# Channel attention through the channel products of the normalised image instead of through queries and keys of every pixel

## The chip, the cores and the metric

The kernel runs on one core of a Trainium2 chip. The metric is the time of one execution on the device, in microseconds. The kernel is one program of four layers that run one after the other on the same core; the change touches the third of them, `layer2`.

## The reference, cut to what matters

```python
# x: 8 images, 384 channels, 32 x 32 pixels; four layers, each x = x + layer(_gn(x)); this is the third
def _L2_conv_ref(x, w_qkv, temperature, w_out, b_out):
    xt = x.reshape(b, c, n).transpose(0, 2, 1)              # n = 1024 pixels, c = 384
    q, k, v = jnp.split(xt @ w_qkv, 3, axis=-1)
    q = q.reshape(b, n, h, d).transpose(0, 2, 1, 3)         # h = 8 heads, d = 48
    k = k.reshape(b, n, h, d).transpose(0, 2, 3, 1)
    v = v.reshape(b, n, h, d).transpose(0, 2, 1, 3)
    q = q / jnp.maximum(jnp.sqrt(jnp.sum(q * q, axis=-2, keepdims=True)), 1e-12)
    k = k / jnp.maximum(jnp.sqrt(jnp.sum(k * k, axis=-1, keepdims=True)), 1e-12)
    k = k * temperature
    attn = jax.nn.softmax(jnp.einsum('bhpn,bhnq->bhpq', k, q), axis=-1)   # 48 x 48 per head
    out = jnp.einsum('bhnp,bhpq->bhnq', v, attn)
    out = out.transpose(0, 2, 1, 3).reshape(b, n, c) @ w_out + b_out
    return out.transpose(0, 2, 1).reshape(b, c, H, W)
```

The attention is over channels. All that it takes from queries and keys are three sets of sums over the pixels: k with q, k with k, and q with q, head by head. `_gn` is a group normalisation without weights (32 groups); its mean and scale for each channel come from sums that the layer before has left in `stat`.

## The kernel before, in words

`layer2` starts with `norm_params`, which turns `stat` into a mean and a scale for each channel (`gn`), while SyncE loads image 0 and the weights (`begin`) and GpSimd clears tiles (`fill`). Then the main block goes through the 8 images. Everything is float32. The 384 channels lie as 3 groups of 128 partitions (`G3`); an image is 1024 pixels, 8 chunks of 128 (`NT`).

For each image, in the order of the data:

- VectorE normalises `xs` into `h` (L645, three instructions).
- TensorE projects (`project`, L838): for each chunk of pixels and for keys and queries in turn, three matmuls of 384 columns into one of four PSUM banks `p_a`. That is a "fill", 16 of them an image; ScalarE copies each to `kq` (L811). TensorE waits for the copy of fill i-4 before fill i.
- TensorE sums over the pixels (L849): for each head 8 matmuls of `kq` with itself, 112 columns wide (k in columns 0 to 47, q in 64 to 111), into `gram` in the two banks `p_g`.
- VectorE takes the diagonals of kk and qq (L743, L745, L749), a matmul with ones (L854) spreads the query sums, ScalarE takes square roots (L817, L819), VectorE divides and scales (L752 to L767), and the softmax follows (L770 to L778, with ScalarE's exponential at L822).
- TensorE transposes the 8 small matrices (L859), mixes them with `w_out` (L870, two steps for each half), and multiplies with the value weights (L877) to `f`, a 384 x 384 matrix for this image. VectorE copies the stages out of PSUM (L780, L784, L788).
- TensorE applies `f` to `h` (L885, 18 matmuls of 512 columns), VectorE adds bias and residual into `xo` (L793) and leaves the sums for the next layer (L798). SyncE stores `xo`.

The order on TensorE is written out by hand: while the attention chain of image b runs on the other engines, the projection of image b+1 is fed in between, cut at `BEFORE` = 3, 9, 11 and 12 fills. The loop runs over pairs of images with two buffers each for `xs` and `h`. In the last turn it wraps around, so the normalisation and projection of image 0 are made once more and not used. The load of image b+1 is issued on SyncE only when the previous image has been written to `xo` (L717), since it takes over its buffer, and VectorE normalises image b+1 at the head of turn b (L735 to L737), ahead of the attention chain of image b. `Arena.loop_sem` is a semaphore that starts at one, for waits in a hardware loop; `sem_inc` on `tick` counts and nothing waits for it.

Of the kernel before, what the change touches and what calls it, by code (L numbers as in the profile page):

```python
# [654 lines left out]
def layer2(nc, sh, x, w_qk, w_vT, w_out, temp, b_out, y):  # L655
# [5 lines left out]
    yv = y.rearrange("b (g p) n -> p b g n", p=P)  # L661
    with Arena(nc, "c") as a:
        xs = a.sb("xs", [P, 2, G3, N])
        h = a.sb("h", [P, 2, G3, N])
# [24 lines left out]
        s_sub, s_an, s_tt, s_te, s_m, s_me, s_f, s_fe, s_o, s_oe, s_st = (
            a.loop_sem(n) for n in ("sub", "an", "tt", "te", "m", "me", "f", "fe", "o", "oe", "st"))  # L690
        a.open()


        BEFORE = (3, 9, 11, 12)
        def begin(e):
            e.dma_start(xs[:, 0, :, :], xv[:, 0, :, :]).then_inc(s_x[0].sem, 16)
            e.dma_start(w[:], w_qk.rearrange("(g p) s n -> p g s n", p=P)).then_inc(s_w.sem, 16)
# [3 lines left out]
            e.dma_start(bo[:], b_out.rearrange("(g p) -> p g", p=P), allow_slow_non_contiguous=True).then_inc(s_w.sem, 16)  # L701

        def fill(e):
            e.memset(kq[:], 0.0).then_inc(s_z.sem, 1)
            e.memset(ones[:], 1.0).then_inc(s_z.sem, 1)
            e.memset(m[:], 0.0).then_inc(s_z.sem, 1)
            e.wait_ge(s_z.sem, s_z.at(3))

        norm_params(nc, sh, "n2", p_a[0], begin, fill)
        with nc.Block() as block:  # L710

            @block.sync
            def _(e):
                with e.Fori(0, B // 2) as b2:
                    for u in range(2):
                        b = b2 * 2 + u
                        e.wait_ge(s_oe.sem, s_oe.at(b * 6))  # L717
                        e.sem_inc(sh["tick"], 1)
                        e.dma_start(xs[:, 1 - u, :, :].unsqueeze(1), xv[:, ds((b + 1) % B, 1), :, :]).then_inc(s_x[1 - u].sem, 16)
                        e.wait_ge(s_oe.sem, s_oe.at(b * 6 + 6))  # L720
                        e.dma_start(yv[:, ds(b, 1), :, :], xo[:].unsqueeze(1)).then_inc(s_y.sem, 16)
                        e.wait_ge(s_y.sem, s_y.at((b + 1) * 16))
                        e.sem_inc(s_yd.sem, 1)
                for u in range(2):
                    e.wait_ge(s_x[u].sem, s_x[u].at(16 * (B // 2 + 1 - u)))

            @block.vector
            def _(e):
                e.wait_ge(s_x[0].sem, s_x[0].at(16))
                normalise(e, sh, h[:, 0, :, :], xs[:, 0, :, :], 0).then_inc(s_h.sem, 1)  # L730
                e.wait_ge(s_w.sem, s_w.at(80))
                with e.Fori(0, B // 2) as b2:
                    for u in range(2):
                        b = b2 * 2 + u
                        e.wait_ge(s_x[1 - u].sem, s_x[1 - u].at((b2 + 1 + u) * 16))  # L735
                        e.wait_ge(s_o.sem, s_o.at(b * 6))
                        normalise(e, sh, h[:, 1 - u, :, :], xs[:, 1 - u, :, :], (b + 1) % B).then_inc(s_h.sem, 1)  # L737

                        e.wait_ge(s_g.sem, s_g.at(b + 1))
                        idk = sh["ident"][0:D, 0:D].unsqueeze(1).broadcast_to([D, 4, D])  # L740
                        idq = sh["ident"][64:TP, 64:TP].unsqueeze(1).broadcast_to([D, 4, D])
                        for v in range(2):
                            e.tensor_tensor(dq[64:TP, 4 * v:4 * v + 4, :], gram[64:TP, v, :, 64:TP], idq, ALU.mult).then_inc(s_dq.sem, 1)  # L743
                        for v in range(2):
                            last = e.tensor_tensor(dk[:, 4 * v:4 * v + 4, :], gram[0:D, v, :, 0:D], idk, ALU.mult)  # L745
                        last.then_inc(s_c.sem, 1)
                        e.wait_ge(s_c.sem, s_c.at(b * 5 + 1))
                        e.sem_inc(sh["tick"], 1)
                        e.tensor_reduce(rk[:], dk[:], AX, ALU.add).then_inc(s_dq.sem, 1)  # L749

                        e.wait_ge(s_sq.sem, s_sq.at(b * 2 + 1))
                        e.tensor_scalar(rk[:], rk[:], 1e-12, None, ALU.max)  # L752
                        e.wait_ge(s_sq.sem, s_sq.at(b * 2 + 2))
                        e.tensor_scalar(rq[:], rq[:], 1e-12, None, ALU.max).then_inc(s_c.sem, 1)
                        e.wait_ge(s_c.sem, s_c.at(b * 5 + 2))
                        e.sem_inc(sh["tick"], 1)
                        e.reciprocal(rk[:], rk[:])
                        e.reciprocal(rq[:], rq[:]).then_inc(s_c.sem, 1)
                        e.wait_ge(s_c.sem, s_c.at(b * 5 + 3))
                        e.sem_inc(sh["tick"], 1)  # L760
                        e.tensor_tensor(rk[:], rk[:], tmp[:], ALU.mult)
                        for v in range(2):
                            last = e.tensor_tensor(at2[:, 4 * v:4 * v + 4, :], gram[0:D, v, :, 64:TP], rq[:, 4 * v:4 * v + 4, :], ALU.mult)
                        last.then_inc(s_c.sem, 1)
                        e.wait_ge(s_c.sem, s_c.at(b * 5 + 4))
                        e.sem_inc(sh["tick"], 1)
                        e.tensor_tensor(at2[:], at2[:], rk[:].unsqueeze(2).broadcast_to([D, HEADS, D]), ALU.mult).then_inc(s_c.sem, 1)  # L767
                        e.wait_ge(s_c.sem, s_c.at(b * 5 + 5))
                        e.sem_inc(sh["tick"], 1)
                        e.tensor_reduce(mx[:], at2[:], AX, ALU.max).then_inc(s_sub.sem, 1)  # L770
                        e.wait_ge(s_sub.sem, s_sub.at(b * 4 + 1))
                        e.tensor_tensor(at2[:], at2[:], mx[:].unsqueeze(2).broadcast_to([D, HEADS, D]), ALU.subtract).then_inc(s_sub.sem, 1)
                        e.wait_ge(s_ex.sem, s_ex.at(b + 1))
                        e.tensor_reduce(mx[:], at2[:], AX, ALU.add).then_inc(s_sub.sem, 1)
                        e.wait_ge(s_sub.sem, s_sub.at(b * 4 + 3))
                        e.reciprocal(mx[:], mx[:]).then_inc(s_sub.sem, 1)
                        e.wait_ge(s_sub.sem, s_sub.at(b * 4 + 4))
                        e.tensor_tensor(at2[:], at2[:], mx[:].unsqueeze(2).broadcast_to([D, HEADS, D]), ALU.mult).then_inc(s_an.sem, 1)  # L778
                        e.wait_ge(s_tt.sem, s_tt.at(b + 1))
                        e.tensor_copy(attT[:].rearrange("p h d -> p (h d)"), p_m[0:D, 0, 0:C]).then_inc(s_te.sem, 1)  # L780
                        for v in range(PAIRS):
                            e.wait_ge(s_m.sem, s_m.at(b * 4 + v + 1))
                            for r in (0, 64):
                                last = e.tensor_copy(m[r:r + D, v, :], p_m[r:r + D, v % 2, 0:C])  # L784
                            last.then_inc(s_me.sem, 1)
                        for g in range(G3):
                            e.wait_ge(s_f.sem, s_f.at(b * 3 + g + 1))
                            e.tensor_copy(f[:, g, :], p_a[g][:, 0:C]).then_inc(s_fe.sem, 1)  # L788
                        e.wait_ge(s_yd.sem, s_yd.at(b))
                        for i in range(2 * G3):  # L790
                            g, n = i // 2, i % 2
                            e.wait_ge(s_o.sem, s_o.at(b * 6 + i + 1))
                            e.scalar_tensor_tensor(xo[:, g, n * HALF:(n + 1) * HALF], p_a[i % 4][:], bo[:, g:g + 1],  # L793
                                                   xs[:, u, g, n * HALF:(n + 1) * HALF], ALU.add, ALU.add).then_inc(s_oe.sem, 1)
# [8 lines left out]
            def _(e):  # L803
                def leave(n, steps):

                    for i in steps:
                        c, s = i // 2, i % 2
                        e.wait_ge(s_a.sem, s_a.at(n * (2 * NT) + i + 1))
                        if i == 0:
                            e.wait_ge(s_g.sem, s_g.at(n))  # L810
# [1703 lines left out]
```

## Time and profile before

| | |
|---|---|
| median of 3 runs | 6763.02 us (6761.66 to 6776.2) |
| profiled execution | 6760.66 us, its span 6758.4 us |
| TensorE matmul busy, whole span | 5974.2 us (88%) |
| `layer2`, from its first instruction to that of the layer after it | 5641.9 to 6327.4 us of the span |
| TensorE matmul busy in one image of `layer2` (5766.8 to 5845.3) | 74.03 of 78.50 us |
| VectorE, ScalarE busy in the same image | 25.70, 12.50 us |

All times within the span are in microseconds from its start. A float32 matmul stands in the trace as two instructions, so the 48 matmuls of a projection are x96; a transpose stands as one. Matmuls are pipelined: the duration of one is longer than the distance to the next.

### The profile page before, as it was taken

Reading aid. Unit: us, or ns where it says so; the run is one execution under the profiler, and the core shown is the slowest. Engines: PE = TensorE matmul, PEld = TensorE weight load, DVE = VectorE, ACT = ScalarE, POOL = GpSimd, SP = SyncE. Lnnn points to the kernel's source line nnn. Section 1 sums busy time; section 2 is a strip of 40 time slices with the busy share of each in tenths; the row PEclk is TensorE's granted clock in tenths of the full one; section 3 lists DMA queues with packets and bytes.
Section 4 is the critical chain, followed back from the end, with each engine's and each line's share of the span. In section 5 each row is a group of like instructions: output and inputs, shape, how many; then the busy total and the mean of one; then the engine's idle time right before and its main releaser. Section 6 shows DMA issues by size and latency. Waiting matters only on the chain. (4 is left out here: it accounts for less than half of the span.)

```text
span 6758.4 us, 123692 instructions
## 1 busy us (share of the span) xinstructions
PE 5974.2 (88%) x46612; PEld 4080.9 (60%) x46612; DVE 4837.0 (72%) x10092; ACT 3924.4 (58%) x5363; POOL 783.3 (12%) x780
## 2 busy tenths in 40 slices
PE   5999999999968989988889889898898996999798
PEld 2554454445425558865578755688556884555598
DVE  6877787788755779877788777888678893333333
ACT  3766676676633558865578755787556882111242
POOL 2212222221220011000020100100101100000000
PEclk9999999999989989999989999999998998999899
DMA  4111112111114545545355544454545552101598
GB/s 141 45 53 55 40 48 58 54 39 43 45 58 118 117 103 127 120 104 122 88 133 123 121 103 109 115 126 107 124 103 121 115 121 78 38 37 56 125 231 200
DMA packets 198795, 652.65 MB, mean 97 GB/s; under 512 B 61769, under 2 KB 68865, under 8 KB 155315
## 3 DMA queue, kind: packets, MB, share of 16 engines
q1 hardware_dynamic: 178147, 606.02, 36.5%
q0 software_dynamic: 19968, 37.78, 2.1%
q8 instruction: 400, 6.55, 0.4%
q14 instruction: 280, 2.29, 0.1%
HBM read 539.94 MB, written 65.59 MB: 90 GB/s over the span
## 5 line engine op out<-in xcount | busy, mean ns | idle before, releaser
L2330 PE MATMUL b_p<-b_work,b_hkt 64*128 64x144 f32 (+37 forms) x27520 | 2113.6, 309 | 257.1 <-DVE b_acc L2201 148.9
L2330 PEld LDWEIGHTS b_p<-b_work,b_hkt 64*128 64x128 f32 x27520 | 1964.9, 195 | 482.2 <-DVE b_work L2276 282.9
L2276 DVE TENSOR_TENSOR b_work<-b_work 128x140 f32<-128x140 f32 (+26 forms) x5312 | 1610.5, 356 | 230.1 <-PE b_p L2330 175.9
L2171 ACT ACTIVATE b_work<-b_work,b_mcol 128x512 f32<-128x512 f32 (+6 forms) x1328 | 764.8, 647 | 1025.3 <-DVE b_work L2276 886.0
L530 ACT ACTIVATE a_ex<-a_p_t 128x1024 f32<-128x1024 f32 x512 | 523.8, 1023 | 420.0 <-PE a_p_t L466 417.4
L2175 ACT ACTIVATE b_work<-b_work,b_mrow 128x544 f32<-128x544 f32 (+6 forms) x1328 | 762.1, 645 | 0.0
L2201 DVE SCALAR_TENSOR_TENSOR b_acc<-b_p,b_dwc,b_acc 128x323 f32<-128x323 f32 (+14 forms) x1088 | 624.2, 577 | 184.2 <-PE b_p L2330 184.2
L596 DVE TENSOR_REDUCE a_nm<-a_p_x 128x1 f16<-128x1024 f32 x512 | 624.8, 1220 | 147.4 <-PE a_p_x L455 138.5
L1742 PE MATMUL b_p<-b_hp,b_ow 128*98 128x512 f32 x1568 | 723.5, 612 | 0.0
L602 DVE TENSOR_TENSOR a_el<-a_ex,a_eh 128x1024 f16<-128x1024 f32 x512 | 680.7, 1330 | 6.7 <-ACT a_eh L535 6.7
L535 ACT CAST a_eh<-a_ex 128x1024 f16<-128x1024 f32 x512 | 535.5, 1046 | 54.7 <-ACT a_ex L530 3.0
L2210 DVE SCALAR_TENSOR_TENSOR b_acc<-b_p,b_dwc,b_acc 128x1024 f32<-128x1024 f32 x384 | 491.4, 1280 | 91.3 <-PE b_p L2330 89.7
L2178 ACT ACTIVATE b_work<-b_work 128x1792 f32<-128x1792 f32 (+2 forms) x332 | 530.9, 1599 | 0.0
L1742 PEld LDWEIGHTS b_p<-b_hp,b_ow 128*98 128x98 f32 x1568 | 251.5, 166 | 398.7 <-issue 394.0
L466 PE MATMUL a_p_t<-a_q,a_kh 97*128 97x512 f16 x1024 | 393.7, 384 | 34.0 <-ACT a_ex L530 34.0
L484 PE MATMUL a_p_o<-a_eh,a_v 128*112 128x512 f16 x1024 | 397.9, 389 | 26.8 <-DVE a_osum L590 19.3
L2180 ACT ACTIVATE b_work<-b_work 128x736 f32<-128x736 f32 (+13 forms) x332 | 396.0, 1193 | 0.0
L484 PE MATMUL a_p_o<-a_el,a_v 128*112 128x512 f16 x1024 | 394.8, 386 | 0.0
L455 PE MATMUL a_p_x<-a_kh,a_q 96*128 96x512 f16 x1024 | 315.9, 390 | 88.8 <-DVE a_nm L596 88.1
L466 PE MATMUL a_p_t<-a_q,a_kl 96*128 96x512 f16 x1024 | 393.4, 384 | 0.0
L1770 POOL TENSOR_TENSOR b_off<-b_off,b_grid 18x512 f32<-18x512 f32 (+2 forms) x56 | 79.4, 1418 | 2262.8 <-DVE b_mx L1763 2262.8
L1739 PE MATMUL b_p<-b_halves,b_ows 128*114 128x512 f16 (+1 forms) x1360 | 325.3, 391 | 13.9 <-DVE b_halves L1834 10.1
(212 smaller groups left out, 6059.0 us busy)
## 6 DMA issues: line engine op xcount, KB each, us to landing
b_work<-sampling_positions SPq DMA_DIRECT2D x666, 512.0 KB, 6.5
d_win<-merged_kernels SPq DMA_DIRECT2D x192, 263.0 KB, 7.0
b_xin<-x SPq DMA_DIRECT2D x24, 1024.0 KB, 9.6
a_xr<-in_x SPq DMA_DIRECT2D x12, 1536.0 KB, 10.0
x<-a_xr SPq DMA_DIRECT2D x9, 1536.0 KB, 6.1
c_xs<-x SPq DMA_DIRECT2D x9, 1536.0 KB, 6.4
b_xr<-x SPq DMA_DIRECT2D x13, 1024.0 KB, 18.8
x<-b_xr SPq DMA_DIRECT2D x13, 1024.0 KB, 4.7
```

The lines of the kernel that those rows point to most:

```text
L466: last = e.matmul(p_t[:, n, :], kk[0:r, hd, c * P:(c + 1) * P], q[0:r, hd, n * HALF:(n + 1) * HALF], start=(r > MAXROW), stop=(r == MAXROW))
L484: last = e.matmul(bank[0:TP, :], v[:, c, hh % HEADS, :], part[:, k % WR, n * HALF:(n + 1) * HALF], start=(c == 0 and r == 0), stop=(c == N ...
L535: e.copy(eh[:, m % WR, :], ex[:, m % ER, :]).then_inc(s_e.sem, 1)
L596: e.tensor_reduce(nm[:, k // NT % 4, k % NT:k % NT + 1], p_x[:].rearrange("p a n -> p (a n)"), AX, ALU.max, negate=True).then_inc(s_m.sem, 1)
L602: e.tensor_tensor(el[:, k % WR, :], ex[:, k % ER, :], eh[:, k % WR, :], ALU.subtract).then_inc(s_l.sem, 1)
L1742: last = e.matmul(bank_of(u[1])[0:M, :].rearrange("p (a b) -> p a b", b=W), ow[:, k * M:(k + 1) * M], hp[:, s, r0:r0 + 16, c0:c0 + W], sta ...
L2171: last = e.activation(rx[:, u, xo[c]:xo[c + 1]].rearrange("p (a b) -> p a b", a=H), pp[:, b, 1, :].rearrange("p (a b) -> p a b", a=H)[:, : ...
L2175: last = e.activation(ry[:, u, yo[c]:yo[c + 1]], pp[:, b, 0, first_row * W:end * W], ACT.Abs, bias=mrow[:, c:c + 1])
L2178: e.activation(rx[:, u, 0:xo[SIDE]], rx[:, u, 0:xo[SIDE]], ACT.Relu, bias=1.0, scale=-1.0).then_inc(tp.s_rx.sem, 1)
L2201: e.scalar_tensor_tensor(total, G, dwc[:, g, tap:tap + 1], total, ALU.mult, ALU.add).then_inc(tp.s_g.sem, 1)
L2276: e.tensor_tensor(S[:, k % NS, 0:(r1 - r0) * w].rearrange("p (a b) -> p a b", b=w), rx[:, u, xo[cc]:xo[cc + 1]].rearrange("p (a b) -> p a ...
L2330: last = e.matmul(G[:, a0 - top:z0 - top, c0 - left:c1 - left], hkt[64 * s:64 * s + 64, SIDE * cr + cc, :], S[64 * s:64 * s + 64, k % NS, ...
```

## The change

In place of q and k for all pixels, the kernel computes the 384 x 384 products of the normalised image with itself, summed over the pixels, and multiplies the weights on both sides of them: with H = h h^T, the sums of keys with queries are Wk^T H Wq, and likewise the other two.

- The work of image b+1 that is fed in between ("ahead", with `FILLS` = 18 steps) is now: 8 fills that transpose the pixel chunks of `h`, three 128x128 blocks each, copied by ScalarE to `hT`; the products (`GRAM`, steps 8 to 10), 8 chunks of three matmuls of 384, 256 and 128 columns, so that only the upper blocks are made; `MIRROR` (step 11), three transposes for the lower blocks; and 6 fills (`PRODUCT`) of H with the query and key weights, three matmuls of 384 columns each, copied to `hw`.
- The sums for the attention (`gram`) are then 3 matmuls a head of the weights with `hw`, 112 columns wide, 24 an image instead of 64.
- The weights `w` are laid out by head with gaps (112 columns a head), 1344 KB instead of 1152 KB.
- `xs` and `h` have three buffers. Images 1 and 2 are loaded in `begin`, image b+2 when image b-1 has been written to `xo`. VectorE normalises image b+2 in turn b after the copy to `attT`, ahead of the copies of `m`.
- The 8 images are unrolled, with no hardware loop; the wrapped work of the last turn is gone, and so are the increments of `tick`. VectorE waits for the store itself (`s_y`).
- The matmuls to `f` write to `p_f` (the `p_g` banks and one of `p_m`) and no longer to `p_a`, so they no longer wait for the fills; the last two fills now stand between them and the output matmuls.
- The fills are divided anew: steps 0 to 2, 3 to 10, 11 to 13, 14, 15, then 16 and 17.

The lines taken out stand in the listing above; of the diff, the new lines with what surrounds them:

```diff
+    RING = 3
+    TURNS, GRAM, MIRROR, PRODUCT = 0, NT, NT + G3, NT + G3 + 1
+    FILLS = PRODUCT + 2 * G3
...
+        xs = a.sb("xs", [P, RING, G3, N])
+        h = a.sb("h", [P, RING, G3, N])
+        w = a.sb("w", [P, G3, HEADS, TP])
...
+        hT = a.sb("hT", [P, NT, C])
+        hh = a.sb("hh", [P, G3, C])
+        hw = a.sb("hw", [P, G3, HEADS, TP])
...
+        p_f = (p_g[:, 0, 0:C], p_g[:, 1, 0:C], p_m[:, 0, 0:C])
...
+        def load(e, b):
+            e.dma_start(xs[:, b % RING, :, :], xv[:, b, :, :]).then_inc(s_x[b % RING].sem, 16)
...
+                for b in range(B):
+                    if 0 < b < B - 2:
                         e.wait_ge(s_oe.sem, s_oe.at(b * 6))
+                        load(e, b + 2)
+                    e.wait_ge(s_oe.sem, s_oe.at(b * 6 + 6))
+                    e.dma_start(yv[:, b, :, :], xo[:]).then_inc(s_y.sem, 16)
+                e.wait_ge(s_y.sem, s_y.at(16 * B))
...
+                def normalised(b):
+                    u = b % RING
+                    e.wait_ge(s_x[u].sem, s_x[u].at((b // RING + 1) * 16))
+                    if b >= RING:
+                        e.wait_ge(s_o.sem, s_o.at((b - RING + 1) * 6))
+                    normalise(e, sh, h[:, u, :, :], xs[:, u, :, :], b).then_inc(s_h.sem, 1)
+
+                normalised(0)
+                normalised(1)
...
+                    for i in steps if n < B else ():
+                        e.wait_ge(s_a.sem, s_a.at(n * FILLS + i + 1))
+                        bank = p_a[i % 4]
+                        if i < GRAM:
+                            last = e.copy(hT[:, i, :], bank[:, 0:C])
+                        elif i < MIRROR:
+                            g = i - GRAM
+                            last = e.copy(hh[:, g, g * P:C], bank[:, 0:C - g * P])
+                        elif i == MIRROR:
+                            e.copy(hh[:, 1, 0:P], bank[:, 0:P])
+                            last = e.copy(hh[:, 2, 0:2 * P], bank[:, P:3 * P])
+                        else:
+                            o, s = 2 - (i - PRODUCT) // 2, (i - PRODUCT) % 2
+                            last = e.copy(hw[:, o, :, 64 * s:64 * s + D], bank[:, 0:C].rearrange("p (h d) -> p h d", h=HEADS))
+                        last.then_inc(s_ae.sem, 1)
+
+                leave(0, range(FILLS))
+                for b in range(B):
+                    leave(b + 1, range(0, 3))
                     e.wait_ge(s_dq.sem, s_dq.at(b * 3 + 3))
                     e.activation(rk[:], rk[:], ACT.Sqrt).then_inc(s_sq.sem, 1)
                     e.wait_ge(s_qq.sem, s_qq.at(b + 1))
                     e.activation(rq[:].rearrange("p h d -> p (h d)"), p_m[0:D, 0, 0:C], ACT.Sqrt).then_inc(s_sq.sem, 1)
+                    leave(b + 1, range(3, GRAM))
                     e.wait_ge(s_sub.sem, s_sub.at(b * 4 + 2))
                     e.activation(at2[:], at2[:], ACT.Exp).then_inc(s_ex.sem, 1)
+                    leave(b + 1, range(GRAM, FILLS))
...
+                def ahead(n, steps):
+                    for i in steps if n < B else ():
+                        bank, u = p_a[i % 4], n % RING
                         if i == 0:
                             e.wait_ge(s_h.sem, s_h.at(n + 1))
+                            if n > 1:
                                 e.wait_ge(s_oe.sem, s_oe.at((n - 1) * 6))
                         if i >= 4:
+                            e.wait_ge(s_ae.sem, s_ae.at(n * FILLS + i - 3))
+                        if i < GRAM:
+                            for g in range(G3):
+                                last = e.transpose(bank[:, g * P:(g + 1) * P], h[:, u, g, i * P:(i + 1) * P], sh["ident"][:])
+                            last.then_inc(s_a.sem, 1)
+                        elif i == GRAM:
+                            e.wait_ge(s_ae.sem, s_ae.at(n * FILLS + GRAM - 1))
+                            for c in range(NT):
+                                if c == NT - 1:
+                                    e.wait_ge(s_ae.sem, s_ae.at(n * FILLS + GRAM))
+                                for g in range(G3):
+                                    last = e.matmul(p_a[g][:, 0:C - g * P], hT[:, c, g * P:(g + 1) * P], hT[:, c, g * P:C], start=(c == 0), stop=(c == NT - 1))
+                                    if c == NT - 1:
+                                        last.then_inc(s_a.sem, 1)
+                        elif i == MIRROR:
+                            e.wait_ge(s_ae.sem, s_ae.at(n * FILLS + MIRROR))
+                            for j, (g, o) in enumerate(((0, 1), (0, 2), (1, 2))):
+                                last = e.transpose(bank[:, j * P:(j + 1) * P], hh[:, g, o * P:(o + 1) * P], sh["ident"][:])
+                            last.then_inc(s_a.sem, 1)
+                        elif i >= PRODUCT:
+                            o, s = 2 - (i - PRODUCT) // 2, (i - PRODUCT) % 2
+                            e.wait_ge(s_ae.sem, s_ae.at(n * FILLS + (MIRROR if o == 2 else PRODUCT)))
+                            for g in range(G3):
+                                last = e.matmul(bank[:, 0:C].rearrange("p (h d) -> p h d", h=HEADS), hh[:, g, o * P:(o + 1) * P],
+                                                w[:, g, :, 64 * s:64 * s + D], start=(g == 0), stop=(g == G3 - 1))
+                            last.then_inc(s_a.sem, 1)
+                def mixed(b, vs):
+                    for v in vs:
+                        if v >= 2:
+                            e.wait_ge(s_me.sem, s_me.at(b * 4 + v - 1))
+                        for s in range(2):
+                            last = e.matmul(p_m[64 * s:64 * s + D, v % 2, 0:C], attT[:, 2 * v + s, :], wo[:, 2 * v + s, :], start=True, stop=True)
+                        last.then_inc(s_m.sem, 1)
+                e.wait_ge(s_w.sem, s_w.at(80))
+                ahead(0, range(FILLS))
+                for b in range(B):
+                    u = b % RING
+                    e.wait_ge(s_ae.sem, s_ae.at((b + 1) * FILLS))
+                    if b:
+                        e.wait_ge(s_fe.sem, s_fe.at(b * 3))
+                    for hd in range(HEADS):
                         for g in range(G3):
+                            last = e.matmul(gram[0:TP, hd // 4, hd % 4, :], w[:, g, hd, :], hw[:, g, hd, :], start=(g == 0), stop=(g == G3 - 1))
+                    last.then_inc(s_g.sem, 1)
+                    ahead(b + 1, range(0, 3))
+                    e.wait_ge(s_dq.sem, s_dq.at(b * 3 + 2))
+                    e.matmul(p_m[0:D, 0, 0:C], ones[64:TP, :], dq[64:TP, :, :].rearrange("p h d -> p (h d)"), start=True, stop=True).then_inc(s_qq.sem, 1)
+                    ahead(b + 1, range(3, MIRROR))
+                    e.wait_ge(s_an.sem, s_an.at(b + 1))
+                    for hd in range(HEADS):
+                        last = e.transpose(p_m[0:D, 0, hd * D:(hd + 1) * D], at2[:, hd, :], sh["ident"][0:D, 0:D])
+                    last.then_inc(s_tt.sem, 1)
+                    ahead(b + 1, range(MIRROR, PRODUCT + 2))
+                    e.wait_ge(s_te.sem, s_te.at(b + 1))
+                    mixed(b, range(0, 2))
+                    ahead(b + 1, range(PRODUCT + 2, PRODUCT + 3))
+                    mixed(b, range(2, 4))
+                    ahead(b + 1, range(PRODUCT + 3, PRODUCT + 4))
+                    e.wait_ge(s_me.sem, s_me.at(b * 4 + 4))
+                    for g in range(G3):
                         for v in range(PAIRS):
+                            last = e.matmul(p_f[g], wvT[:, v, g * P:(g + 1) * P], m[:, v, :], start=(v == 0), stop=(v == PAIRS - 1))
+                        last.then_inc(s_f.sem, 1)
+                    ahead(b + 1, range(PRODUCT + 4, FILLS))
+                    if b + 1 < B:
+                        e.wait_ge(s_ae.sem, s_ae.at((b + 2) * FILLS))
+                    e.wait_ge(s_fe.sem, s_fe.at(b * 3 + 3))
+                    for i in range(2 * G3):
+                        o, n = i // 2, i % 2
+                        if i >= 4:
+                            e.wait_ge(s_oe.sem, s_oe.at(b * 6 + i - 3))
                         for g in range(G3):
+                            last = e.matmul(p_a[i % 4][:], f[:, g, o * P:(o + 1) * P], h[:, u, g, n * HALF:(n + 1) * HALF], start=(g == 0), stop=(g == G3 - 1))
+                        last.then_inc(s_o.sem, 1)
```

## Rows read from the trace of the kernel before

**Rows 1.** Timeline, start of layer2: start, duration, engine, line, [idle before, what ended it].
```profile
5641.90 1.28 ACT L170 ACT_TABLE_LOAD   x1 [26.37 <-PEq L70]
...
5659.82 0.50 PEld L838 LDWEIGHTS c_p_a<-c_w,c_h 128*128 128x128 f32 x2 [9.96 <-DMA c_bo<-in_c_bo]
```
**Rows 2.** Windows (length, busy by engine, clock, DMA): start, projection 0, images 1, 7.
```profile
5641.90:5659.80 17.90, 1.96 (x12) 1.75 (x12) 7.94 (x35) 1.49 (x2) 7.46 (x3) 0.50 0.94 280
5659.80:5693.20 33.40, 32.84 (x96) 18.95 (x96) 2.26 (x3) 7.67 (x16) 0.00 (x0) 0.95 0.05 19
...
5766.80:5845.30 78.50, 74.03 (x311) 43.99 (x310) 25.70 (x45) 12.50 (x22) 0.00 (x0) 0.98 0.11 41
6238.00:6323.10 85.10, 75.65 (x311) 44.52 (x309) 30.11 (x52) 12.51 (x22) 0.00 (x0) 0.95 0.13 51
```
**Rows 3.** Timeline, TensorE: the sums over pixels of images 0 and 7.
```profile
5693.23 12.84 PE L849 MATMUL c_p_g<-c_kq 128*112 128x112 f32 x128 [0.57 <-ACT c_kq L811]
...
6237.98 12.75 PE L849 MATMUL c_p_g<-c_kq 128*112 128x112 f32 x128
```
**Rows 4.** Timeline, images 1 and 7: the wait for the next normalised image.
```profile
5780.33 2.26 DVE L645 TENSOR_SCALAR c_h<-c_xs,gn 128x1024 f32<-128x1024 f32 x3 [8.75 <-DMA c_xs<-x]
...
5782.72 7.67 PE L838 MATMUL c_p_a<-c_w,c_h 128*128 128x384 f32 x18 [3.16 <-DVE c_h L645]
...
6254.22 9.14 PE L838 MATMUL c_p_a<-c_w,c_h 128*128 128x384 f32 x18 [3.49 <-DVE c_h L645]
```
**Rows 5.** Windows in and behind that wait of image 1, columns as in rows 2.
```profile
5779.50:5782.70 3.20, 0.06 (x1) 0.00 (x0) 2.33 (x4) 0.00 (x0) 0.00 (x0) 0.98 0.00 0
...
5784.70:5785.70 1.00, 1.00 (x3) 0.60 (x2) 0.00 (x0) 0.00 (x0) 0.00 (x0) 0.50 0.00 0
```
**Rows 6.** Timeline, ScalarE: a copy that waits for its fill, and two in succession.
```profile
5667.54 0.48 ACT L811 COPY c_kq<-c_p_a 128x384 f32<-128x384 f32 x1 [1.46 <-PE c_p_a L838]
...
5709.41 1.06 ACT L811 COPY c_kq<-c_p_a 128x384 f32<-128x384 f32 x2
```
**Rows 7.** Timeline, image 0: the attention chain and the matmuls behind it.
```profile
5707.53 0.55 DVE L749 TENSOR_REDUCE c_rk<-c_dk 48x8 f32<-48x384 f32 x1 [0.15 <-DVE c_dk L745]
...
5713.83 0.47 ACT L819 ACTIVATE c_rq<-c_p_m 48x384 f32<-48x384 f32 x1
...
5719.70 0.55 DVE L772 TENSOR_TENSOR c_att<-c_att,c_mx 48x384 f32<-48x384 f32 x1
...
5724.45 0.39 PEld L859 LDWEIGHTS c_p_m<-ident,c_att 48*48 48x48 f32 x8 [0.60 <-issue]
...
5728.98 1.49 PE L870 MATMUL c_p_m<-c_wo,c_attT 48*48 48x384 f32 x8
...
5729.87 2.28 DVE L784 COPY c_m<-c_p_m 48x384 f32<-48x384 f32 x4 [4.31 <-PE c_p_m L870]
...
5733.96 8.01 PE L838 MATMUL c_p_a<-c_w,c_h 128*128 128x384 f32 x24
...
5742.61 8.00 PE L877 MATMUL c_p_a<-c_m,c_wvT 112*128 112x384 f32 x24 [0.64 <-ACT c_kq L811]
...
5751.26 15.72 PE L885 MATMUL c_p_a<-c_h,c_f 128*128 128x512 f32 x36 [0.65 <-DVE c_f L788]
...
5767.92 3.66 DVE L798 BATCH_NORM_STATS2 stat<-c_xo 128x512 f32 x6 [0.15 <-DVE c_xo L793]
```
**Rows 8.** Timeline, layer 3: 128x128 transposes at either clock.
```profile
6347.41 1.09 PE L1184 MATMUL d_bank<-ident,d_h 128*128 128x128 f32 x8 [1.23 <-DVE d_h L1096]
6350.02 1.97 PE L1184 MATMUL d_bank<-ident,d_h 128*128 128x128 f32 x8 [1.52 <-DVE d_h L1096]
```
**Rows 9.** The transposes of layer 3, one line: duration ns min/median/max.
```profile
L1184 PE MATMUL d_bank<-ident,d_h x192: 272/273/477, 6342.8 to 6610.2; 128*128 128x128 f32 x192
```
**Rows 10.** Window of layer 3 with transposes alone, columns as in rows 2.
```profile
6345.00:6346.00 1.00, 1.00 (x7) 0.94 (x5) 0.97 (x3) 0.84 (x3) 0.00 (x0) 0.61 1.01 416
```
**Rows 11.** Groups by line: weight loads of the sums over pixels (busy, mean ns).
```profile
L849 PEld LDWEIGHTS c_p_g<-c_kq 128*112 128x112 f32 x1024 | 101.9, 178 | 4.6 <-issue 3.4 <-ACT c_kq L811 1.2
```

More of the change, by code:

```diff
@@ L701, in begin @@
             e.dma_start(bo[:], b_out.rearrange("(g p) -> p g", p=P), allow_slow_non_contiguous=True).then_inc(s_w.sem, 16)
+            for b in range(1, RING):
+                load(e, b)
         def fill(e):
-            e.memset(kq[:], 0.0).then_inc(s_z.sem, 1)
+            e.memset(hw[:], 0.0).then_inc(s_z.sem, 1)
             e.memset(ones[:], 1.0).then_inc(s_z.sem, 1)
@@ L731, in _ @@
-                e.wait_ge(s_w.sem, s_w.at(80))
[L732 to L794, printed above, removed]
-                        e.wait_ge(s_oe.sem, s_oe.at(b * 6 + 6))
-                        for i in range(2 * G3):
-                            g, n = i // 2, i % 2
-                            last = e.bn_stats(one(sh["stat"][:, g, ds(b, 1), n, :]), xo[:, g, n * HALF:(n + 1) * HALF])
-                        last.then_inc(s_st.sem, 1)
@@ new lines, in _ @@
+                idq = sh["ident"][64:TP, 64:TP].unsqueeze(1).broadcast_to([D, 4, D])
+                for b in range(B):
+                    u = b % RING
+                    e.wait_ge(s_g.sem, s_g.at(b + 1))
+                    for v in range(2):
+                        e.tensor_tensor(dq[64:TP, 4 * v:4 * v + 4, :], gram[64:TP, v, :, 64:TP], idq, ALU.mult).then_inc(s_dq.sem, 1)
+                    for v in range(2):
+                        last = e.tensor_tensor(dk[:, 4 * v:4 * v + 4, :], gram[0:D, v, :, 0:D], idk, ALU.mult)
+                    last.then_inc(s_c.sem, 1)
+                    e.wait_ge(s_c.sem, s_c.at(b * 5 + 1))
+                    e.tensor_reduce(rk[:], dk[:], AX, ALU.add).then_inc(s_dq.sem, 1)
+                    e.wait_ge(s_sq.sem, s_sq.at(b * 2 + 1))
+                    e.tensor_scalar(rk[:], rk[:], 1e-12, None, ALU.max)
+                    e.wait_ge(s_sq.sem, s_sq.at(b * 2 + 2))
+                    e.tensor_scalar(rq[:], rq[:], 1e-12, None, ALU.max).then_inc(s_c.sem, 1)
+                    e.wait_ge(s_c.sem, s_c.at(b * 5 + 2))
+                    e.reciprocal(rk[:], rk[:])
+                    e.reciprocal(rq[:], rq[:]).then_inc(s_c.sem, 1)
+                    e.wait_ge(s_c.sem, s_c.at(b * 5 + 3))
+                    e.tensor_tensor(rk[:], rk[:], tmp[:], ALU.mult)
+                    for v in range(2):
+                        last = e.tensor_tensor(at2[:, 4 * v:4 * v + 4, :], gram[0:D, v, :, 64:TP], rq[:, 4 * v:4 * v + 4, :], ALU.mult)
+                    last.then_inc(s_c.sem, 1)
+                    e.wait_ge(s_c.sem, s_c.at(b * 5 + 4))
+                    e.tensor_tensor(at2[:], at2[:], rk[:].unsqueeze(2).broadcast_to([D, HEADS, D]), ALU.mult).then_inc(s_c.sem, 1)
+                    e.wait_ge(s_c.sem, s_c.at(b * 5 + 5))
+                    e.tensor_reduce(mx[:], at2[:], AX, ALU.max).then_inc(s_sub.sem, 1)
+                    e.wait_ge(s_sub.sem, s_sub.at(b * 4 + 1))
+                    e.tensor_tensor(at2[:], at2[:], mx[:].unsqueeze(2).broadcast_to([D, HEADS, D]), ALU.subtract).then_inc(s_sub.sem, 1)
+                    e.wait_ge(s_ex.sem, s_ex.at(b + 1))
+                    e.tensor_reduce(mx[:], at2[:], AX, ALU.add).then_inc(s_sub.sem, 1)
+                    e.wait_ge(s_sub.sem, s_sub.at(b * 4 + 3))
+                    e.reciprocal(mx[:], mx[:]).then_inc(s_sub.sem, 1)
+                    e.wait_ge(s_sub.sem, s_sub.at(b * 4 + 4))
+                    e.tensor_tensor(at2[:], at2[:], mx[:].unsqueeze(2).broadcast_to([D, HEADS, D]), ALU.mult).then_inc(s_an.sem, 1)
+                    e.wait_ge(s_tt.sem, s_tt.at(b + 1))
+                    e.tensor_copy(attT[:].rearrange("p h d -> p (h d)"), p_m[0:D, 0, 0:C]).then_inc(s_te.sem, 1)
+                    if b + 2 < B:
+                        normalised(b + 2)
+                    for v in range(PAIRS):
+                        e.wait_ge(s_m.sem, s_m.at(b * 4 + v + 1))
+                        for r in (0, 64):
+                            last = e.tensor_copy(m[r:r + D, v, :], p_m[r:r + D, v % 2, 0:C])
+                        last.then_inc(s_me.sem, 1)
+                    for g in range(G3):
+                        e.wait_ge(s_f.sem, s_f.at(b * 3 + g + 1))
+                        e.tensor_copy(f[:, g, :], p_f[g]).then_inc(s_fe.sem, 1)
+                    e.wait_ge(s_y.sem, s_y.at(16 * b))
+                    for i in range(2 * G3):
+                        g, n = i // 2, i % 2
+                        e.wait_ge(s_o.sem, s_o.at(b * 6 + i + 1))
+                        e.scalar_tensor_tensor(xo[:, g, n * HALF:(n + 1) * HALF], p_a[i % 4][:], bo[:, g:g + 1],
+                                               xs[:, u, g, n * HALF:(n + 1) * HALF], ALU.add, ALU.add).then_inc(s_oe.sem, 1)
+                    e.wait_ge(s_oe.sem, s_oe.at(b * 6 + 6))
+                    for i in range(2 * G3):
+                        g, n = i // 2, i % 2
+                        last = e.bn_stats(sh["stat"][:, g, b, n, :], xo[:, g, n * HALF:(n + 1) * HALF])
+                    last.then_inc(s_st.sem, 1)
@@ L804, in leave @@
                 def leave(n, steps):
[L806 to L810, printed above, removed]
-                        e.copy(kq[:, c, :, 64 * s:64 * s + D], p_a[i % 4][:, 0:C].rearrange("p (h d) -> p h d", h=HEADS)).then_inc(s_ae.sem, 1)
-                leave(0, range(2 * NT))
-                with e.Fori(0, B) as b:
-                    leave(b + 1, range(0, BEFORE[0]))
+                    for i in steps if n < B else ():
[16 more added lines that the diff above has]
+                    leave(b + 1, range(0, 3))
                     e.wait_ge(s_dq.sem, s_dq.at(b * 3 + 3))
@@ L834, in project @@
                                 e.wait_ge(s_oe.sem, s_oe.at((n - 1) * 6))
                         if i >= 4:
-                            e.wait_ge(s_ae.sem, s_ae.at(n * (2 * NT) + i - 3))
-                        for g in range(G3):
-                            last = e.matmul(p_a[i % 4][:, 0:C], h[:, u, g, c * P:(c + 1) * P], w[:, g, s, :], start=(g == 0), stop=(g == G3 - 1))
-                        last.then_inc(s_a.sem, 1)
-                e.wait_ge(s_w.sem, s_w.at(80))
-                project(0, 0, range(2 * NT))
@@ L2485, in laid_out @@
     w = i["L2_conv_w_qkv"].reshape(C, 3, C)
-    t["c_wqk"] = w[:, 1::-1]
+    wqk = np.zeros((C, HEADS, 2, 64), f)
+    wqk[..., 0:D] = w[:, 1::-1].reshape(C, 2, HEADS, D).transpose(0, 2, 1, 3)
+    t["c_wqk"] = wqk.reshape(C, HEADS, 128)[..., 0:TP]
     wv = np.zeros((PAIRS, 2, 64, C), f)
```

81 lines of the change are left out of this document (10 added, 71 removed).

## The prediction

> **What bounds the kernel now.** The table of the page comes first: TensorE is busy 88% of the span, and in one image of `layer2` 74.0 of 78.5 us, while VectorE works 25.7 and ScalarE 12.5 [rows 2]. So I read the layer as a stream of matmuls: its time is the matmuls' distances from start to start, plus what the others make TensorE wait. Next the timeline, image by image. The sums over pixels of image 0 start at 5693.2 and those of image 7 at 6238.0, seven images in 544.8 us [rows 3]; one in the steady part takes 78.5. It contains one real stall: at the head of each turn TensorE has 3.16 us without work, because the next image was loaded late and VectorE normalises it only then (VectorE itself sat 8.75 us for the load) [rows 4]. In that gap the granted clock falls to 0.50, 1.2 GHz, and stays there into the next fills [rows 5]. Three fills at full clock take 3 x 1.94 = 5.8 us (a fill is 1.94 us, the copy's idle and busy time in rows 6), and here the group lasts 7.7 and in image 7 even 9.1 [rows 4]. That is 1.7 to 3.2 us on top of the stall.
>
> **Prices.** Of one matmul instruction (half a float32 matmul): 384 columns 1.94/6 = 0.3225 us [rows 6]; 112 columns 12.75/128 = 0.0996 [rows 3]; 256 columns, by proportion to 384, 0.215. A 128x128 transpose is (1.09 - 0.27)/7 = 0.117 us at full clock, with 0.27 for the last one's own length, and (1.97 - 0.48)/7 = 0.213 at half [rows 8, 9]. I take 0.117 for a half of 128 columns too; proportion gives 0.107. Copies of a fill in succession go at 1.06 - 0.48 = 0.58 us each [rows 6].
>
> **One image after, from the start of the attention sums to the next.**
> (a) The sums: 24 matmuls, 48 x 0.0996 = 4.8 us, where 12.75 stood.
> (b) Until the products can start: this stretch is set by ScalarE. TensorE needs three transposes a fill, 0.35 us, but each fill must be copied in 0.58, and the square roots lie between. Three copies end 2.4 us after the sums. The reduction of rk ends 2.0 after them (5708.1 against 5706.1 in the old image 0) [rows 3, 7]. The table load of 1.28 [rows 1] and two square roots bring 4.3. The copies of fills 3 to 6 end at 6.6, where the products begin, with fill 7 copied before their last chunk. TensorE has 8 x 0.35 + 0.8 of work in these 6.6 us and waits nearly 3.
> (c) The products: 8 x 2 x (0.3225 + 0.215 + 0.117) = 10.5. The attention chain, 9.9 us from the square roots to the weights (5714.3 to 5724.3) [rows 7] and so over at about 14, hides behind (b) and (c).
> (d) ScalarE's last copies of the products before the mirror can read them, with the small transposes beside: 0.95.
> (e) Mirror 0.35, two fills 3.87, then the mixing with a fill in it 4.98 (5728.98 to 5733.96) [rows 7], a fill 1.94 and 0.1 for VectorE's last copy of m: 11.3. The copy begins 0.9 after the second mixing and takes 2.3 [rows 7]; 1.4 of mixing and 1.94 of fill just cover it.
> (f) To f 12 x 0.645 = 7.7, two fills 3.87, the wait for the last copy 0.9 (four fills, 7.74, stand in the 8.65 from 5733.96 to 5742.61), output 15.55 [rows 7, 3]: 28.05. The old wait of 0.65 for the copies of f goes under the two fills.
> Sum 62.2. The stall at the head goes: images are loaded and normalised a turn ahead, VectorE's 2.3 us lie where it has time.
>
> **The clock** is the open term. In the second half of (b) TensorE has little to do, and an idle stretch of 3.2 us was enough for the fall to 0.50 [rows 5]. After a fall the rows show 1.7 to 3.2 us lost. I expect a fall in most images, partly spent in waiting anyway, and put in 1.5: 63.7 an image. Bounds: nothing, as where no gap is near, and 3.2.
> The Trainium skill ("TensorE: Matmul & The Clock Gate", Part 4) says that full clock does not engage for transposes since they do not count as busy. By that rule all of (b) but its one ones-matmul is idle, the fall is certain, and the 1.5 becomes about 3. The trace disagrees in part: with nothing but transposes in succession the clock rose, 0.61 on the way from 0.50 to 1 [rows 10], but the looser ones behind stayed slow [rows 8].
>
> **First projection.** The weights hold TensorE until 5659.8 [rows 1]. They grow by 192 KB, at 280 GB/s [rows 2] 0.7 us. Then 5.0 of transposes at ScalarE's pace, 10.5, 0.95, 0.35, six fills 11.6, 0.9 for the last copy, and 1.9 for the cold clock as now (32.84 against 16 x 1.94): 31.2 where 33.4 was [rows 2]. Net -1.5. The smaller clearing of `hw` on GpSimd lies ahead of the weights and is worth nothing. Unknown is whether the two images now queued behind the weights slow them: nothing if served in order, (3.1 MB at some 300 GB/s) 10 us if shared evenly. That the last weight ends the wait [rows 1], and not the longest, speaks for order: I take nothing and keep 10.
>
> **Seven images:** 7 x 63.7 = 445.9 against 544.8, -98.9.
>
> **The last image** has no next one to fill in, and the wrapped projection is gone. Before, it takes 85.1 us to the end of its statistics [rows 2]. After: sums 4.8; square roots done 2.75 later, since the table load can stand ahead of the wait (as L170's does, at the very start of its block) [rows 1]; to the subtraction 5.95; exponential 0.55 and the rest of the softmax 1.4: 10.65. Small transposes and their copy 1.3, the four mixings in step with the copies of m 5.5: 17.5. From L877 to L885 8.65, from there to the last statistics 20.3 [rows 7]: 46.5. The long idle time costs clock again, 2.5 (between 1.7 and 3.2). 4.8 + 46.5 + 2.5 = 53.8, so -31.3. If the table loads come behind the waits, +2.6.
>
> **Sum:** -1.5 - 98.9 - 31.3 = -131.7. The profiled execution took 6760.7, so 6629.0; the median of the runs is 2.3 above it, so 6631. What lies in front of `layer2` and behind it is not touched. Costed at nothing: `tick`, the semaphores, the longer straight code (short matmuls held 0.0996 each over 128 in succession [rows 3]), the two buffers more, and the ScalarE load at L811, which goes with the loop. If it stayed, (b) would be 1.3 longer, +9 in all.
>
> **Rivals.**
> *The clock stays up.* Then (b) costs no more than its waits: -10.5, 6620. For it: waits of 0.9 and 0.65 in the old image cost no clock, and the idle time in (b) is broken in two by a fill. Against it: rows 5. Chance 0.15.
> *The clock falls early and comes back late in every image,* 3.2 lost instead of 1.5: +12, 6643. For it: image 7 in rows 4, and the rule above. Chance 0.15.
> *Loading the stationary side sets the pace of the short matmuls.* A load lasts 0.178 us [rows 11]; if the 16 short halves of the products and the mirror took 0.19 and not 0.117, 1.4 an image, +11; with the eight transposing fills as well, up to +25: 6642 to 6656. Against it: the same 0.178 went with a pace of 0.0996. Chance 0.08.
> *The start is slowed by the two images:* +10, 6641. Chance 0.07.
> *Slower than before: the clock does not come back at all in (b) to (f).* Its place is the ring of four banks: three quick transposes, a wait for ScalarE, again and again, then a product that starts cold. All matmuls at 1.2 GHz would add some 55 us an image, to about 7070. It turns the sign once more than 131.7/8 = 16.5 us an image are lost, that is with over 33 us of matmuls at half clock. Against it: in rows 4 and 5 the clock came back within the first group of fills, and (c) alone is 10.5 without a wait. Chance 0.02.
> That the change does nothing is excluded: by the prices above it takes away 13.7 us of matmuls an image (8.0 at the sums; 31.0 of projection against 25.3 of transposes, products, mirror and fills), and TensorE had only the 3.2 of stall in which to lose them.
>
> **How the numbers follow.** My forecast, 6631 give or take 9, has 0.53. The range goes from the clock that stays up, with a few microseconds of copies quicker than costed, 6612, to the early fall with slow loads or the slow start, 6656; outside it lie about 0.2. A measurement tells 0.2%, some 14 us, from no change; every case but the last is at least 100 us below 6763. Faster 0.97, same 0.01, slower 0.02.
>
> **What would show it.** Distance from one start of the attention sums to the next near 63 to 64; those sums 4.8 long; transposes paced by copies at 0.58; products from 6.6 after the sums, first part at clock 0.50; no wait for `c_h`; the last image 54 to the end of its statistics. The prediction is wrong if the distance is over 67: then see whether the products' short matmuls or the clock took it, or a wait at the mixing, where VectorE now normalises before it copies m.

## The result, and the profile after

The changed kernel takes 6602.9 us (median of 4 runs, 6595.3 to 6608.0) against 6763.3 before: a ratio of 0.976, 95% interval 0.9745 to 0.9774. It is faster, as forecast, but by 160 us where 132 were forecast, and below the range, which ended at 6612. The profiled execution took 6607.0, its span 6604.7.

The page of the profile gives TensorE the same 88% as before, so it decides nothing:

```profile
PE 5836.1 (88%) x45996; PEld 3998.1 (61%) x45996; DVE 4831.0 (73%) x10089; ACT 3905.2 (59%) x5362; POOL 782.4 (12%) x780
```

The windows of the layer, in the order of [rows 2]: start, first fills, image 2, last image.

```profile
5650.10:5669.50 19.40, 1.96 (x12) 1.74 (x12) 5.60 (x35) 1.49 (x2) 3.73 (x3) 0.50 0.96 273
5669.50:5698.40 28.90, 27.45 (x111) 19.43 (x111) 2.26 (x3) 8.01 (x19) 0.00 (x0) 0.93 0.18 73
...
5818.40:5878.80 60.40, 58.41 (x246) 34.91 (x245) 25.54 (x45) 11.16 (x24) 0.00 (x0) 1.00 0.15 53
...
6120.40:6174.50 54.10, 37.92 (x135) 18.89 (x133) 27.79 (x49) 2.39 (x4) 0.00 (x0) 0.84 0.13 51
```

An image takes 60.4 us instead of 78.5, and the granted clock (third number from the right) is 1.00 through all of it. The layer's marks are the starts of four instructions: its first, the attention sums of image 0, those of image 7, and the first of the next layer. They give the parts of all kernels of this study, in us; "one image" is a seventh of "seven images":

| kernel | start | seven images | one image | last image to the next layer | `layer2` |
|---|---|---|---|---|---|
| before | 51.3 | 544.8 | 77.8 | 89.4 | 685.5 |
| changed | 48.3 | 421.9 | 60.3 | 57.8 | 528.0 |
| e1, old mathematics | 52.5 | 507.3 | 72.5 | 66.6 | 626.3 |
| e2, two buffers | 47.5 | 496.3 | 70.9 | 58.7 | 602.4 |
| e3, copied twice | 49.1 | 452.6 | 64.7 | 57.6 | 559.2 |
| e4, copied fourfold | 57.8 | 492.3 | 70.3 | 58.9 | 609.0 |
| e5, early start | 38.8 | 421.9 | 60.3 | 57.5 | 518.2 |
| e6, fills first | 47.9 | 410.4 | 58.6 | 58.6 | 516.9 |
| e7, all three | 38.6 | 404.5 | 57.8 | 57.7 | 500.8 |

The layer is 157.4 us shorter, -3.0, -122.9 and -31.6 in its parts. Outside it the two profiled executions differ by +8.2 before and -4.5 behind, where nothing was changed; the runs of one kernel spread by 3 to 22 us. So the layer's length is the finer measure, and the table is read rather than the totals.

One image after, TensorE alone (start, duration, engine and line; L892 attention sums, L851 transposing fills, L896 the ones, L859 products, L900 the small transposes, L865 mirror, L911 the matmuls to f, L922 output):

```profile
5818.43 4.88 PE L892 MATMUL c_p_g<-c_hw,c_w 128*112 128x112 f32 x48
5823.15 1.15 PE L851 MATMUL c_p_a<-ident,c_h 128*128 128x128 f32 x9
5824.22 0.84 PE L896 MATMUL c_p_m<-c_dq,c_ones 48*48 48x384 f32 x2
5824.99 1.53 PE L851 MATMUL c_p_a<-ident,c_h 128*128 128x128 f32 x12
5827.23 0.55 PE L851 MATMUL c_p_a<-ident,c_h 128*128 128x128 f32 x3 [0.70 <-ACT c_hT L813]
5828.44 10.64 PE L859 MATMUL c_p_a<-c_hT 128*128 128x384 f32 x48 [0.67 <-ACT c_hT L813]
5839.01 0.52 PE L900 MATMUL c_p_m<-ident,c_att 48*48 48x48 f32 x8
5839.58 0.52 PE L865 MATMUL c_p_a<-ident,c_hh 128*128 128x128 f32 x3
...
5850.92 5.33 PE L911 MATMUL c_p_g<-c_m,c_wvT 112*128 112x384 f32 x16
...
5863.26 15.72 PE L922 MATMUL c_p_a<-c_h,c_f 128*128 128x512 f32 x36 [0.57 <-ACT c_hw L822]
5878.81 4.88 PE L892 MATMUL c_p_g<-c_hw,c_w 128*112 128x112 f32 x48
```

From start to start: (a) 4.7, forecast 4.8; (b) from 5823.15 to the products 5.3, forecast 6.6; (c) and (d) to the mirror 11.1, forecast 11.45; (e) to the matmuls for f 11.3, forecast 11.3; (f) to the next sums 27.9, forecast 28.05. Two waits of 0.7 are all that is left in (b), where nearly 3 us were forecast. ScalarE in image 1 says why:

```profile
5763.28 1.24 ACT L813 COPY c_hT<-c_p_a 128x384 f32<-128x384 f32 x3 [20.85 <-PE c_p_a L851]
...
5764.54 1.28 ACT L829 ACT_TABLE_LOAD   x1
...
5766.32 1.96 ACT L813 COPY c_hT<-c_p_a 128x384 f32<-128x384 f32 x5
```

Copies in succession overlap: each lasts 0.48, and five of them end (1.96 - 0.48)/4 = 0.37 us after each other, not 0.58.

### The profile page after: what moved, and what is told of

The parts are those of the page before. It is cut to its first block and busy times, and to the rows that moved or that the text cites. A ratio compares the mean times of both kernels' runs of the same rounds, so it can differ in the third digit from the quotient of the medians.

```text
span 6604.7 us, 121718 instructions
## 1 busy us (share of the span) xinstructions
PE 5836.1 (88%) x45996; PEld 3998.1 (61%) x45996; DVE 4831.0 (73%) x10089; ACT 3905.2 (59%) x5362; POOL 782.4 (12%) x780
## 5 line engine op out<-in xcount | busy, mean ns | idle before, releaser
L1776 PE MATMUL b_p<-b_halves,b_ows 128*114 128x512 f16 (+1 forms) x1360 | 325.3, 391 | 13.9 <-DVE b_halves L1871 10.1
```

## The experiments

**e1, the old mathematics in the new frame.** It separates buffers and unrolling from the products.

```diff
-    FILLS = PRODUCT + 2 * G3
+    FILLS = 2 * NT                      # kq, w and the sums over pixels as before the change
...
-                    ahead(b + 1, range(3, MIRROR))
+                    ahead(b + 1, range(3, 9))
```

> All of the change but its mathematics: three buffers, images unrolled, loads and normalisation a turn ahead, f in other banks, no wrapped projection, but queries and keys of all pixels are projected and summed as before. Theory A (the gain is the stall, the cold clock behind it and the wrapped turn, plus fewer matmuls, each in its own place): the old image 0, which had no stall, took 73.6 us, and 0.65 of wait for f goes under fills, so 73 us from one start of the sums to the next where the kernel before has 78.5 and the changed one 60.4; the last image 62; layer2 about 628 long against 685 and 528, so 6763 - 57 = 6706, and the mathematics alone is worth some 100 us. Rival B (unrolled code or the earlier loads do more than that, for instance in the start of the layer): under 71 us an image. Rival C (the buffers bring nothing without the new mathematics, since the load is still late): 76 or more.

6703.4 (6698.6 to 6709.8), ratio 0.992, interval 0.9902 to 0.9935. The layer is 626.3 long, 72.5 an image; theory A holds to within 3 us, B and C fall. The clock is 1.00 in its image:

```profile
5842.30:5914.70 72.40, 71.83 (x311) 43.20 (x310) 25.53 (x45) 11.21 (x21) 0.00 (x0) 1.00 0.13 44
```

So of the 157 us the frame brings 59 (37.5 over seven images, 22.8 at the end, -1.1 at the start) and the mathematics 98; these shares hold for this order of the two steps. The parts of the frame were not tested one by one with the old sums. The stall, the cold clock behind it and the wait for f, 3.16, 1.7 and 0.65 in [rows 4] and [rows 7], come to 5.5 of its 6.0 an image.

**e2, the new mathematics with two buffers.** The load (with its wait for the store) and the normalisation are where they were.

```diff
-    RING = 3
+    RING = 2
...
-                    if b + 2 < B:
-                        normalised(b + 2)          # after attT
+                    if b + 1 < B:
+                        normalised(b + 1)          # at the head of the turn
```

> The new mathematics, unrolled, with two buffers: the load of the next image is issued after the previous output and its store, and VectorE normalises at the head of the turn, as before the change. Theory A: the next image is normalised 15.8 us after the start of the sums, as in the trace of before, but the new sums last only 4.7, so the stall at the head grows from 3.2 to 11 us and the clock falls in it: 72.5 to 74.5 us an image instead of 60.4, about 6690 to 6700. Rival B: the third buffer is worth no more than it removed before (3.2 us and 1.7 of clock): 65 us an image, 6635.

6674.9 (2 runs, 6666.2 and 6683.5), ratio 0.987, interval 0.9853 to 0.9893. The first of the seven distances is 59.5, the others are 72.4 to 73.4. The wait at the head, 3.16 us before [rows 4], is 10.1:

```profile
5846.49 2.18 PE L849 MATMUL c_p_a<-ident,c_h 128*128 128x128 f32 x9 [10.08 <-DVE c_h L645]
```

Theory A holds for the distance, B falls. The total lies below the 6690 that A named, since only six of the seven distances have the stall: 6602.9 + 6 x 12 is 6675. With shorter sums the same late load makes a stall three times as long: without the third buffer and the early loads the new mathematics gives 83 of the 157 us.

**e3 and e4, slower copies.** Each transposed fill is copied into an unused tile (in float16) as well, once or three times; such a copy goes at the same 0.37.

```diff
                         if i < GRAM:
+                            for j in range(1):     # 3 in e4
+                                e.copy(pad[:, j, i, :], bank[:, 0:C])
                             last = e.copy(hT[:, i, :], bank[:, 0:C])
```

> Each transposed fill is copied once more by ScalarE into a tile that nobody reads, so the ring of four banks goes at 0.75 us a fill instead of 0.37. Theory A (the forecast's idea of the clock: a thin stretch of transposes lets it fall, and the changed kernel escaped only because its copies were quick): products start 7.8 us after the sums instead of 5.3, and the clock is at 0.50 when they start: 2.5 + 1.7 to 3.2 us an image more, 6640 or more. Rival B (transposes count as work and the clock needs a gap without any matmul): only the 2.5, clock 1.00 throughout, about 6624.

> The same with three more copies of each transposed fill, 1.49 us a fill: TensorE works 0.35 us in each 1.5. Products start about 13 us after the sums. Theory A: the clock is at 0.50 for the first microseconds of the products in every image: 7.8 + 1.7 to 3.2 an image more, 6675 or more. Rival B: the clock stays at 1.00, 6665.

6636.8 and 6683.7 (one run each). In e3 the total lies between the two theories (6624 for B, 6640 or more for A) and decides nothing; the clock and the length of the products decide, in both, for A. In e3 an image takes 64.7, 4.3 more: 2.6 for the ring, and 1.7 because the products now last 12.3 instead of 10.6. Timeline, then windows around the start of the products:

```profile
5896.46 0.55 PE L854 MATMUL c_p_a<-ident,c_h 128*128 128x128 f32 x3 [2.09 <-ACT c_hT L816]
5898.80 12.32 PE L862 MATMUL c_p_a<-c_hT 128*128 128x384 f32 x48 [1.79 <-ACT c_hT L816]
```

```profile
5896.80:5898.80 2.00, 0.21 (x3) 0.04 (x1) 1.97 (x2) 2.00 (x6) 0.00 (x0) 1.00 0.03 6
5898.80:5900.80 2.00, 2.00 (x6) 1.47 (x7) 1.90 (x6) 1.89 (x3) 0.00 (x0) 0.65 0.00 0
5900.80:5902.80 2.00, 2.00 (x6) 1.30 (x5) 1.34 (x4) 0.52 (x1) 0.00 (x0) 0.50 0.00 0
```

Behind waits of 2.1 and 1.8 the clock falls soon after the products have begun; in the changed kernel, with 0.7 and 0.7, it does not. In e4 it falls earlier, ahead of the products: in the image shown two waits of 0.99, each with three transposes behind it, were enough. It is still low when the products start, and they last 13.6:

```profile
5848.88 0.55 PE L854 MATMUL c_p_a<-ident,c_h 128*128 128x128 f32 x3 [0.99 <-ACT c_hT L816]
5850.41 0.66 PE L854 MATMUL c_p_a<-ident,c_h 128*128 128x128 f32 x3 [0.99 <-ACT c_hT L816]
...
5858.37 13.58 PE L862 MATMUL c_p_a<-c_hT 128*128 128x384 f32 x48 [3.68 <-ACT c_hT L816]
```

```profile
5849.10:5851.10 2.00, 0.98 (x6) 0.39 (x4) 0.00 (x0) 1.98 (x5) 0.00 (x0) 0.90 1.02 403
5851.10:5853.10 2.00, 0.00 (x0) 0.00 (x0) 0.95 (x4) 1.99 (x6) 0.00 (x0) 0.50 0.14 49
```

The slower copies make the waits longer and the whole thin stretch longer too (8.0 us in e3, 5.3 in the changed kernel); these runs do not separate the two.

**e5, e6, e7: what is left.** e5 moves the wait for the weights behind the steps of image 0 that need none; e6 puts all eight transposing fills ahead of the ones and the square roots, on TensorE and ScalarE; e7 does both and lets output i wait only for the fill in its own bank.

```diff
-                e.wait_ge(s_w.sem, s_w.at(80))
-                ahead(0, range(FILLS))
+                ahead(0, range(PRODUCT))
+                e.wait_ge(s_w.sem, s_w.at(80))
+                ahead(0, range(PRODUCT, FILLS))
...
-                    ahead(b + 1, range(0, 3))
+                    ahead(b + 1, range(0, GRAM))
...
-                    if b + 1 < B:
-                        e.wait_ge(s_ae.sem, s_ae.at((b + 2) * FILLS))
...
+                        if i < 2 and b + 1 < B:
+                            e.wait_ge(s_ae.sem, s_ae.at((b + 2) * FILLS - 1 + i))
```

> TensorE waits for the weights only before the first fill that uses them: transposes, products and mirror of image 0 need image 0 alone. Theory A: the first transpose starts when image 0 is normalised, about 10 us after the layer's first instruction instead of 19.4, the weights are there before they are needed, and the start is 9 us shorter: 6594. Rival B: while the weights and two images arrive, copies and matmuls are slowed or the clock is colder, and half of it is lost: 6598 or more.

> All eight transposing fills of the next image go ahead of the matmul with ones and of the square roots. Theory A (the stretch before the products is set by ScalarE's queue: eight copies, one table load and two square roots in a row): products start 3.5 to 3.9 us after the sums instead of 5.3, the attention chain ends 1.5 us later and is still hidden by the products: 1.5 us an image less, 6592. Rival B: the later square roots delay the softmax past the products, and TensorE waits there what it gained: 6603.

> The early start, the fills first, and output i waiting only for the copy of the fill that had its bank (not both). Theory A: 9 us at the start, 1.5 us an image from the fills, 0.6 us an image from the wait of 0.57 before the outputs: 9 + 10.5 + 4 = 23 less, 6580. Rival B: the gains overlap or the clock now falls somewhere, over 6590.

e5: 6597.4 (2 runs); the first transpose starts 10.3 after the layer's first instruction instead of 19.4, and in the table the start is 9.5 shorter, while nothing else moves by more than 0.3. e6: 6592.0 (2 runs); 1.6 less an image over the seven, 0.8 more in the last one. Their totals lie within the spread of the runs from that of the changed kernel, so these two verdicts rest on the parts. The products of e6 start 3.5 us after the sums:

```profile
5811.18 2.78 PE L850 MATMUL c_p_a<-ident,c_h 128*128 128x128 f32 x24
5813.89 0.84 PE L895 MATMUL c_p_m<-c_dq,c_ones 48*48 48x384 f32 x2
5814.67 10.66 PE L858 MATMUL c_p_a<-c_hT 128*128 128x384 f32 x48
5825.26 0.52 PE L899 MATMUL c_p_m<-ident,c_att 48*48 48x48 f32 x8
```

and the small transposes follow the products without a wait, so the later softmax is still hidden. e7: 6574.8 (4 runs, 6574.4 to 6577.4), ratio 0.972, interval 0.9705 to 0.9738, 28 us below the changed kernel; its layer is 27.2 shorter, 9.8, 17.4 and 0.1 by parts, where 23 were expected. Of the 2.6 less in an image after the first, 0.7 stand ahead of the outputs, where the wait is gone. Theory A holds in all three.

## Why the prediction was wrong

The direction and the account of the gain held: e1 and e2 show both halves of it. The forecast for `layer2` was -131.7, the trace has -157.4. Of these 25.7, 24.0 are in the seven images (445.9 forecast, 421.9 measured) and 1.5 at the start.

- **The step that failed: "Copies of a fill in succession go at 1.06 - 0.48 = 0.58 us each".** It measured 0.37. The row of two copies in [rows 6] is not two copies in succession. TensorE ended a fill every 1.94 us then, and the first copy had been held back by a table load. The same stretch with the rows around it:

```profile
5708.11 1.28 ACT L811 ACT_TABLE_LOAD   x1 [14.94 <-PE c_p_a L838]
5709.41 1.06 ACT L811 COPY c_kq<-c_p_a 128x384 f32<-128x384 f32 x2
5711.92 0.48 ACT L811 COPY c_kq<-c_p_a 128x384 f32<-128x384 f32 x1 [1.46 <-PE c_p_a L838]
```

  The third copy starts at 5711.92; one fill earlier is 5709.98, and a copy of 0.48 from there ends where the row of two ends. So the second copy waited about 0.1 for its fill, too short to split the row. I had taken a wait for TensorE into ScalarE's pace. With 0.37 for the six or seven steps of 0.58 that stand before the products, (b) becomes 5.1 to 5.3, and it measured 5.3: 1.3 an image, 9 us over seven. Another 0.9 went in turn 0, where no table load stood ahead of the square roots.
- **The clock, 1.5 an image or 10.5 us.** It measured nothing: the clock is 1.00 through the image. The mechanism exists: e3 brings the pace to 0.75, and the fall appears and costs 1.7 us, at the lower of the bounds of 1.7 to 3.2 from the rows of before. With the pace read rightly, the "nearly 3" of waiting in (b) would have been about 1.7, and the rival of the clock that stays up would have had more than its 0.15. No run has the assumed pace of 0.58, so whether the clock would have fallen there stays open. That rival as I priced it, 6620, still carried the slow copies, which is why the range missed as well. Rows 5 alone could not decide it: their gap is 3.2 us without a matmul, and since the mean clock in it is still 0.98, the fall came at its very end.
- **The first projection** was forecast as 31.2 and took 28.9. The wrong pace did no harm there: the transposes took 5.1, forecast 5.0, because at the low clock TensorE needs 3 x 0.213 = 0.64 a fill, and the copies follow it. Most of the miss is the 1.9 for the cold clock, which was added to a stretch whose length the cold transposes already set. Weights that came 1.5 later than before, and not 0.7, took back 0.8 of it.
- **Small terms.** (c) and (d) were 0.3 too much an image, (f) 0.15; these are some 3 us over seven. (a) and (e) within 0.1.
- **The last image** was forecast as 53.8 to its last statistics and took 54.1 (6120.4 to 6174.5). The table load stood ahead of the wait there (it ran at 6104.8, the square root at 6127.2), as argued from L170.
- **The other rivals.** The short matmuls are not set by the weight loads: 48 instructions of products took 10.6, forecast 10.5. The two images queued behind the weights cost 0.8 beyond the larger weights at most. The case of a kernel slower than before did not occur: even in e4 the products lost only 2.9 an image to the clock.
- **The rule of the Trainium skill** ("TensorE: Matmul & The Clock Gate", Part 4), that full clock does not engage for transposes, is not borne out here for float32 ones. At the cold start of the changed kernel TensorE did transposes alone, after 13.7 us without work, and the clock rose under them:

```profile
5672.50:5673.00 0.50, 0.50 (x4) 0.50 (x3) 0.00 (x0) 0.40 (x1) 0.00 (x0) 0.50 1.03 410
5673.00:5673.50 0.50, 0.50 (x5) 0.50 (x4) 0.48 (x1) 0.44 (x1) 0.00 (x0) 0.61 1.00 401
5673.50:5674.00 0.50, 0.50 (x7) 0.50 (x5) 0.50 (x2) 0.41 (x2) 0.00 (x0) 1.00 1.00 401
```

The first product starts at 5674.6, after the rise. By that rule the products of every image would have begun cold; at 1.7 each, as in e3, an estimated 12 us more than measured over seven. How near the changed kernel, with its two waits of 0.7, is to the fall that e4 shows behind two of 0.99 was not tried.

## What to carry to other kernels

A row that merges several instructions gives their pace only if none of them waited; ask what the producer's pace was before calling it the consumer's. When the work ahead of a late load gets shorter, the same load costs more: the new frame was worth 6 us an image with the old sums (78.5 against 72.5), and the third buffer with its early loads alone 12 with the new (72.4 against 60.4). After an algebraic rewrite, look again at which waits still need to stand where they are: the weights were no longer needed first, and moving that wait, the fills and the wait ahead of the outputs gave 27 us more.

## What the hardware showed unexpectedly

ScalarE's copies of 128x384 from PSUM last 0.48 us each and follow each other in 0.37. TensorE's clock rose from 1.2 to 2.4 GHz during transposes alone. A thin stretch of transposes with two waits of 0.7 kept the clock up in every image; with two of 0.99 (e4), or with 2.1 and 1.8 (e3), it fell. How much of that is the waits and how much the length of the stretch is open.
